# One tile's first layer in three products instead of one: a split chunk whose low part comes from an accumulating DMA

## The chip, the cores and the metric

The kernel runs on one core of a Trainium2 chip (trn2). The metric is the device time in microseconds of one execution; less is better. The core has five engines with queues of their own: PE (TensorE, matrix products), DVE (VectorE) and ACT (ScalarE) for elementwise work, POOL (GpSimd), and SP (SyncE), which here only issues DMAs. They are ordered by semaphores alone. Each engine works through its queue in order, so an instruction that waits holds up all behind it.

## What is computed

Three layers of a compressed interaction network over 512 samples, 32 fields and 64 embedding dimensions. Each layer multiplies its hidden rows with all rows of the input and mixes the products with a weight matrix:

```python
h, outs = x0, []
for i in range(3):
    Wk = Ws[i].reshape(128, h.shape[1], 32)
    xk = relu(einsum('bhd,bmd,ohm->bod', h, x0, Wk) + bs[i][None, :, None])
    if i != 2:
        outs.append(xk[:, :64])
        h = xk[:, 64:]
    else:
        outs.append(xk)
return concatenate([o.sum(axis=-1) for o in outs], axis=1)
```

All is float32. Layer 1 multiplies x0 with itself, so each pair of rows need be formed only once, with the two weights summed; layers 2 and 3 have 64 x 32 pairs.

## The kernel before

**Tiles.** The pairs (sample, dimension) are 32768 columns, cut into 64 tiles of T = 512. A chunk is 128 pairs of rows: 128 partitions by 512 columns, one contraction of PE. Layer 1 has five chunks (C1), layers 2 and 3 have sixteen each, handled in four groups of G = 4; one DVE instruction forms a group's products (128x2048).

**Stages.** The outer loop of every engine runs over i from 0 to 65. Step i does layer 1 of tile i, layer 2 of tile i - 1 and layer 3 of tile i - 2, in this order on PE. I call layer 1's group of four chunks A and its fifth chunk narrow, layer 2's groups B0 to B3 and layer 3's C0 to C3.

**Plain and split groups.** A plain group (A, B2, C2; L375 and L384) is multiplied as float32, for which the trace shows two matmul instructions per chunk. A split group (B0, B1, B3, C0, C1, C3) is multiplied in three float32r products, one matmul per chunk each. DVE writes the product into ZS (L221), ACT copies it rounded into ZH, the high part (L313), and the low part ZL = ZS - ZH is formed by POOL (L291), for B3 by DVE (L228). PE then adds low weight x high (L394), high weight x high (L397) and high weight x low (L400) into the same accumulator, waiting for the low part only ahead of L400.

**Slots.** ZS, ZH and ZL have three slots each (SSLOTS), given out in the order of the split groups. Group n may write ZS when the low part of group n - 3 is formed (L219), and ZH or ZL when PE has used group n - 3 (L311, L289). Plain groups share the two slots of ZW, X has four slots, XD (the row block that layer 1 multiplies X by) two.

**Between the layers.** ACT applies relu to the accumulator (layers 1 and 2: the hidden half to H at L329, the other half to R12 at L332; layer 3: L324). SP spreads H over the partitions with five DMAs (L145, L148), ACT copies it to PSUM (HP, L306), and DVE multiplies it with X. XD is likewise copied into XDP (L300). DVE sums R12 and R3 over the dimension (L237, L242).

**Order.** Each queue is written out by hand. ACT, step i: high B0, high B1, relu of layer 3 (tile i - 3), hidden copy for layer 3, high B3, copy of XD for tile i + 1, high C0, relu of layer 1, high C1, high C3, hidden copy for layer 2, relu of layer 2. DVE, step i: A's product, the narrow product, B0, B1, B2, B3, sum of R12, C0, low part of B3, C1, C2, C3, sum of R3. SP, step i: load XD and X for tile i + 1, spread layer 1's hidden rows of tile i, spread layer 2's of tile i - 1.

## Time and profile before

| | us |
|---|---|
| median of 3 runs (lowest, highest) | 1852.87 (1852.87, 1853.91) |
| the profiled execution | 1851.87 |
| its span, first to last instruction | 1850.1 |
| busy: PE, DVE, POOL, ACT | 1799.3, 1552.2, 1468.3, 1095.6 |
| mean granted clock of PE | 0.996 of full speed |

The span is what the rows below are read from; the profiled execution is 1.8 us longer than its span, and 1.0 below the median of the runs. A time of busy is the union of an engine's instructions, whatever they wait for inside. Matmuls are pipelined and overlap in the rows, so their distance in the chain of work, not their listed length, is what each costs.

### The profile page before, as it was taken

The page shows a single profiled execution, that of the slowest core. Times are in us where ns is not written, and L with a number is a line of the kernel's source. Part 1 is how long each engine was busy: PE and PEld are TensorE (multiplying, and loading weights), DVE is VectorE, ACT ScalarE, POOL GpSimd, SP SyncE. Part 2 cuts the span into 40 slices and gives each one's busy share as a digit, 9 for nine tenths or more (in the row PEclk, how much of TensorE's full clock was granted, in tenths as well). Part 3 has the DMA queues.
Part 4 walks back from the last instruction along what each step waited for, and adds up shares of the span by engine and source line. Part 5 has one row for each costly group of instructions (what it writes and reads, how often), then busy time and mean ns, then how long its engine had stood idle before and what let it go on. Part 6 is the DMA issues. An engine that isn't in the chain of part 4 may idle for free.

```text
span 1850.1 us, 18063 instructions
## 1 busy us (share of the span) xinstructions
PE 1799.3 (97%) x6284; PEld 1184.3 (64%) x6284; DVE 1552.2 (84%) x853; ACT 1095.6 (59%) x899; POOL 1468.3 (79%) x324
## 2 busy tenths in 40 slices
PE   3899999999999999999999999999999999999997
PEld 1566666666666666666666666666666666666665
DVE  3998898898898888888888888888888888988974
ACT  2566656656656666566565665665666666566562
POOL 0788878878878778778778778778778788788786
PEclk9999999999999999999999999999999999999998
DMA  8565455465465564564564564564564554654610
GB/s 201 111 123 121 98 122 116 101 125 114 100 128 107 105 128 105 106 129 103 107 129 102 109 128 99 114 128 93 121 128 92 122 125 92 125 122 95 126 26 20
DMA packets 119513, 205.83 MB, mean 111 GB/s; under 512 B 18816, under 2 KB 19968, under 8 KB 119424
## 3 DMA queue, kind: packets, MB, share of 16 engines
q1 hardware_dynamic: 119424, 204.68, 52.5%
q8 instruction: 51, 0.84, 0.2%
q14 instruction: 38, 0.31, 0.1%
HBM read 153.75 MB, written 0.52 MB: 83 GB/s over the span
## 4 chain that ended last, share of the span: by engine, by line
PE 96%; POOL 1%; DMA 1%; SPq 1%; ACT 1%; DVE 0%; issue 0%; DVEq 0%; POOLq 0%; ACTq 0%
PE ACC L384 24%; PE ACC L400 19%; PE ACC L394 19%; PE ACC L397 19%; PE ACC L375 12%; PE ACC L378 3%; POOL ZL L291 1%; DMA ZS<-in_w 1%; ACT ZH L313 0%; DVE ZS L221 0%; SPq L158 0%; DVE ZW L204 0%; ACT HP L306 0%; DMA H<-H 0%; SPq L139 0%
## 5 line engine op out<-in xcount | busy, mean ns | idle before, releaser
L291 POOL TENSOR_TENSOR ZL<-ZS,ZH 128x2048 fp32r<-128x2048 f32 x320 | 1468.1, 4617 | 372.8 <-ACT ZH L313 372.8
L313 ACT ACTIVATE ZH<-ZS 128x2048 fp32r<-128x2048 f32 x384 | 734.2, 1912 | 536.7 <-PE ACC L400 415.0
L221 DVE TENSOR_TENSOR ZS<-HP,X 128x2048 f32<-128x2048 f32 x384 | 870.5, 2281 | 150.9 <-ACT HP L306 149.6
L394 PE MATMUL ACC<-ZH,WL 128*128 128x512 f32 x1536 | 497.5, 446 | 7.3 <-ACT ZH L313 7.3
L384 PE MATMUL ACC<-ZW,WF 128*128 128x512 f32 x1024 | 460.2, 592 | 0.0
L400 PE MATMUL ACC<-ZL,WH 128*128 128x512 f32 x1536 | 421.7, 396 | 8.4 <-POOL ZL L291 8.3
L397 PE MATMUL ACC<-ZH,WH 128*128 128x512 f32 x1536 | 421.0, 396 | 0.0
L394 PEld LDWEIGHTS ACC<-ZH,WL 128*128 128x128 f32 x1536 | 289.9, 189 | 151.7 <-issue 98.9
L216 DVE TENSOR_TENSOR ZW<-HP,X 128x2048 f32<-128x2048 f32 x128 | 292.2, 2283 | 101.3 <-PE ACC L384 101.3
L400 PEld LDWEIGHTS ACC<-ZL,WH 128*128 128x128 f32 x1536 | 287.9, 188 | 81.6 <-POOL ZL L291 11.7
L397 PEld LDWEIGHTS ACC<-ZH,WH 128*128 128x128 f32 x1536 | 288.8, 188 | 70.2
L384 PEld LDWEIGHTS ACC<-ZW,WF 128*128 128x128 f32 x1024 | 194.0, 189 | 195.1 <-issue 183.7
L375 PE MATMUL ACC<-ZW,W 128*128 128x512 f32 x512 | 233.6, 599 | 30.8 <-DVE ZW L204 30.8
L375 PEld LDWEIGHTS ACC<-ZW,W 128*128 128x128 f32 x512 | 98.2, 192 | 131.1 <-issue 125.5
L204 DVE TENSOR_TENSOR ZW<-XDP,X 128x2048 f32<-128x2048 f32 x64 | 145.6, 2275 | 22.0 <-ACT XDP L300 18.0
L228 DVE TENSOR_TENSOR ZL<-ZS,ZH 128x2048 fp32r<-128x2048 f32 x64 | 157.7, 2464 | 1.4 <-ACT ZH L313 1.4
L324 ACT ACTIVATE R<-ACC,bias_sb 128x512 f32<-128x512 f32 x64 | 44.0, 688 | 170.4 <-PE ACC L400 170.4
L306 ACT ACTIVATE HP<-H 128x1024 f32<-128x1024 f32 x128 | 129.9, 1015 | 9.8 <-DMA H<-H 9.8
L329 ACT ACTIVATE H<-ACC,bias_sb 64x512 f32<-64x512 f32 x128 | 86.6, 676 | 9.4 <-PE ACC L378 5.1
L332 ACT ACTIVATE R<-ACC,bias_sb 64x512 f32<-64x512 f32 x128 | 87.5, 684 | 1.6
L378 PE MATMUL ACC<-ZN,W 128*128 128x512 f32 x128 | 65.4, 592 | 0.0
L237 DVE TENSOR_REDUCE S<-R 128x8 f32<-128x512 f32 (+1 forms) x65 | 43.9, 675 | 2.7 <-ACT R L332 2.7
(32 smaller groups left out, 165.0 us busy)
## 6 DMA issues: line engine op xcount, KB each, us to landing
X<-in_xpad SPq DMA_DIRECT2D x256, 512.0 KB, 9.0
H<-H SPq DMA_DIRECT2D x512, 64.0 KB, 2.0
XD<-in_xpad SPq DMA_DIRECT2D x256, 64.0 KB, 2.0
H<-H SPq DMA_DIRECT2D x128, 128.0 KB, 2.2
ZS<-in_w SPq DMA_DIRECT2D x6, 256.0 KB, 11.4
WF<-in_w SPq DMA_DIRECT2D x2, 256.0 KB, 11.9
out<-XD SPq DMA_DIRECT2D x4, 128.0 KB, 1.8
W<-in_w SPq DMA_DIRECT2D x1, 320.0 KB, 3.0
```

What stands on the lines that cost most here:

```text
L204: nc.vector.tensor_tensor(to, over(XDP[:, :], G), x[:, 0:G, :], ALU.mult).then_inc(wide_ready, 1)
L216: nc.vector.tensor_tensor(wide_slot(i, layer), h, x, ALU.mult).then_inc(wide_ready, 1)
L221: nc.vector.tensor_tensor(ZS[:, n % SSLOTS, :, :], h, x, ALU.mult).then_inc(prod_ready, 1)
L228: nc.vector.tensor_tensor(ZL[:, n % SSLOTS, :, :], ZS[:, n % SSLOTS, :, :], ZH[:, n % SSLOTS, :, :], ALU.subtract).then_inc(low_by_dve, 1)
L291: nc.gpsimd.tensor_tensor(ZL[:, n % SSLOTS, :, :], ZS[:, n % SSLOTS, :, :], ZH[:, n % SSLOTS, :, :], ALU.subtract).then_inc(low_by_pool, 1)
L306: nc.scalar.activation(HP[layer][:, :, :], H[layer][:, :, :], ACT.Copy).then_inc(h_copied[layer], 1)
L313: nc.scalar.activation(ZH[:, n % SSLOTS, :, :], ZS[:, n % SSLOTS, :, :], ACT.Copy).then_inc(high_ready, 1)
L375: last = nc.tensor.matmul(ACC[0][:, :], W1[:, g, :], ZW[:, n % WSLOTS, g, :], start=(g == 0), stop=False)
L384: last = nc.tensor.matmul(ACC[layer][:, :], WF[:, layer - 1, g, :], ZW[:, n % WSLOTS, g, :], start=False, stop=False)
L394: nc.tensor.matmul(ACC[layer][:, :], wl[:, g, :], ZH[:, n % SSLOTS, g, :], start=(k == 0 and g == 0), stop=False)
L397: nc.tensor.matmul(ACC[layer][:, :], wh[:, g, :], ZH[:, n % SSLOTS, g, :], start=False, stop=False)
L400: last = nc.tensor.matmul(ACC[layer][:, :], wh[:, g, :], ZL[:, n % SSLOTS, g, :], start=False, stop=(k == NS - 1 and g == G - 1))
```

## The change

Layer 1's group A becomes a split group. The weights W1 get a high part W1H (ACT) and a low part W1L (DVE) at the start. In each step PE multiplies W1L x ZH and W1H x ZH, then the narrow chunk as before, then waits for A's low part and multiplies W1H x ZL; relu of layer 1 now waits for that.

A's low part is formed in another way than the others. ACT writes ZH and then, from the same ZS, the negated high part into ZL (float32r, scale -1). POOL, ahead of its subtractions of the step, issues a DMA that adds ZS onto ZL in place (1 MB, 128 rows of 2048 elements). Its landing is counted in a semaphore of its slot, and PE, and the DVE product three groups later, wait for that.

There are now seven split groups in a step, A, B0, B1, B3, C0, C1, C3, over the same three slots. A wait on a low part is for that group's own former (POOL, DVE or DMA) rather than for all earlier ones. On ACT A's two copies stand at the head of the step. XD has one buffer in place of two, and SP loads X before XD and waits for XD's copy in between. The weights of layers 2 and 3 are staged in X's slots 2 and 3 in place of ZS, and the outputs in ZW in place of XD. The diff, cut to its core:

```diff
-PLAIN = 2
-SPLIT = (0, 1, 3)
-BY_DVE = ((1, 2),)
-NS = len(SPLIT)
+SPLIT = {0: (0,), 1: (0, 1, 3), 2: (0, 1, 3)}
+PLAIN = {0: (), 1: (2,), 2: (2,)}
+LOW_BY = {
+    (0, 0): "dma",
+    (1, 0): "pool", (1, 1): "pool", (1, 3): "dve",
+    (2, 0): "pool", (2, 1): "pool", (2, 3): "pool",
+}
+NS = 3
...
+        W1H, W1L = sb("W1H", [128, G, OUT], f32r), sb("W1L", [128, G, OUT], f32r)
...
-        XD = sb("XD", [128, 2, T])
+        XD = sb("XD", [128, T])
...
-        WS = ZS[:, 0:2, 0:NS, :].rearrange("p w n (g o) -> p w n g o", g=G)
-        OUTS = XD[:, :, :].rearrange("p a (b c) -> p (a b) c", b=2)
+        WS = X[:, 2:4, 0:NS, :].rearrange("p w n (g o) -> p w n g o", g=G)
+        OUTS = ZW[:, 0, 0:2, :].rearrange("p a (b c) -> p (a b) c", b=2)
...
+        def wait_low(engine, n):
+
+            if LOW_OF[n] == "pool":
+                engine.wait_ge(low_by_pool, LOW_COUNT[n])
+            elif LOW_OF[n] == "dma":
+                engine.wait_ge(low_by_dma[n % SSLOTS], 16 * LOW_IN_SLOT[n])
+            else:
+                engine.wait_ge(low_by_dve, LOW_COUNT[n])
...
                 t = i + 1
                 if live(t):
-                    if t >= 2:
-                        sp.wait_ge(xd_copied, t - 1)
+                    if t == 2:
+                        sp.wait_ge(w_low, 2)
+                    if t >= XSLOTS:
+                        sp.wait_ge(prod_ready, SPLIT_NO[t - XSLOTS + 2, 2, Q - 1] + 1)
+                    load_x(t)
+                    sp.wait_ge(xd_copied, t)
                     load_xd(t)
-                    if t >= XSLOTS:
-                        sp.wait_ge(prod_ready, split_before(t - XSLOTS + 2, 2, NS - 1) + 1)
-                    load_x(t)
...
-            dve.wait_ge(w1_summed, 4)
-
-            def wide_slot(i, layer):
-                n = wide_before(i, layer)
+            dve.wait_ge(w1_high, 1)
+            nc.vector.tensor_tensor(W1L[:, :, :], W1[:, 0:G, :], W1H[:, :, :], ALU.subtract).then_inc(w1_low, 1)
...
             def layer1(i):
                 x = X[:, i % XSLOTS, :, :]
-                to = wide_slot(i, 0)
+                n = SPLIT_NO[i, 0, 0]
+                if n >= SSLOTS:
+                    wait_low(dve, n - SSLOTS)
                 dve.wait_ge(xd_copied, i + 1)
                 dve.wait_ge(x_loaded[i % XSLOTS], 16 * NB * (i // XSLOTS + 1))
-                nc.vector.tensor_tensor(to, over(XDP[:, :], G), x[:, 0:G, :], ALU.mult).then_inc(wide_ready, 1)
+                nc.vector.tensor_tensor(ZS[:, n % SSLOTS, :, :], over(XDP[:, :], G), x[:, 0:G, :],
+                                        ALU.mult).then_inc(prod_ready, 1)
...
-                n = split_before(i, layer, SPLIT.index(q))
+                n = SPLIT_NO[i, layer, q]
                 if n >= SSLOTS:
-                    wait_lows(dve, n - SSLOTS + 1)
+                    wait_low(dve, n - SSLOTS)
                 nc.vector.tensor_tensor(ZS[:, n % SSLOTS, :, :], h, x, ALU.mult).then_inc(prod_ready, 1)
...
+                for layer in range(3):
+                    for q in SPLIT[layer] if live(i - layer) else ():
+                        n = SPLIT_NO[i, layer, q]
+                        if LOW_BY[layer, q] == "dma":
+                            pool.wait_ge(minus_ready, LOW_COUNT[n])
+                            pool.dma_start(ZL[:, n % SSLOTS, :, :], ZS[:, n % SSLOTS, :, :],
+                                           accum_op=ALU.add).then_inc(low_by_dma[n % SSLOTS], 16)
+                        if LOW_BY[layer, q] == "pool":
+                            if n >= SSLOTS:
+                                pool.wait_ge(split_used, n - SSLOTS + 1)
+                            pool.wait_ge(high_ready, n + 1)
+                            nc.gpsimd.tensor_tensor(ZL[:, n % SSLOTS, :, :], ZS[:, n % SSLOTS, :, :],
+                                                    ZH[:, n % SSLOTS, :, :], ALU.subtract).then_inc(low_by_pool, 1)
...
             def high(i, layer, q):
-                n = split_before(i, layer, SPLIT.index(q))
+                n = SPLIT_NO[i, layer, q]
                 if n >= SSLOTS:
                     act.wait_ge(split_used, n - SSLOTS + 1)
                 act.wait_ge(prod_ready, n + 1)
                 nc.scalar.activation(ZH[:, n % SSLOTS, :, :], ZS[:, n % SSLOTS, :, :], ACT.Copy).then_inc(high_ready, 1)
+                if LOW_OF[n] == "dma":
+                    nc.scalar.activation(ZL[:, n % SSLOTS, :, :], ZS[:, n % SSLOTS, :, :], ACT.Copy,
+                                         scale=-1.0).then_inc(minus_ready, 1)
 
             def relu(t, layer):
                 if layer == 0:
-                    act.wait_ge(narrow_used, t + 1)
+                    act.wait_ge(split_used, SPLIT_NO[t, 0, 0] + 1)
...
+            act.wait_ge(w1_summed, 4)
+            nc.scalar.activation(W1H[:, :, :], W1[:, 0:G, :], ACT.Copy).then_inc(w1_high, 1)
+            copy_xd(0)
             for w in range(2):
                 act.wait_ge(ws_loaded[w], 16 * NS)
                 nc.scalar.activation(WH[:, w, :, :, :], WS[:, w, :, :, :], ACT.Copy).then_inc(w_high, 1)
             act.wait_ge(small_loaded, 32)
-            copy_xd(0)
             for i in range(TILES + 2):
+                if live(i):
+                    high(i, 0, 0)
...
-                    pe.wait_ge(w1_summed, 4)
+                    pe.wait_ge(w1_low, 1)
                 else:
                     pe.wait_ge(relu_done[0], i)
-                n = wide_before(i, 0)
-                pe.wait_ge(wide_ready, n + 1)
-                for g in range(G):
-                    last = nc.tensor.matmul(ACC[0][:, :], W1[:, g, :], ZW[:, n % WSLOTS, g, :], start=(g == 0), stop=False)
-                last.then_inc(wide_used, 1)
+                n = SPLIT_NO[i, 0, 0]
+                pe.wait_ge(high_ready, n + 1)
+                for g in range(G):
+                    nc.tensor.matmul(ACC[0][:, :], W1L[:, g, :], ZH[:, n % SSLOTS, g, :], start=(g == 0), stop=False)
+                for g in range(G):
+                    nc.tensor.matmul(ACC[0][:, :], W1H[:, g, :], ZH[:, n % SSLOTS, g, :], start=False, stop=False)
                 pe.wait_ge(narrow_ready, i + 1)
-                nc.tensor.matmul(ACC[0][:, :], W1[:, G, :], ZN[:, :], start=False, stop=True).then_inc(narrow_used, 1)
-
-            def plain(i, layer):
-                n = wide_before(i, layer)
+                nc.tensor.matmul(ACC[0][:, :], W1[:, G, :], ZN[:, :], start=False, stop=False).then_inc(narrow_used, 1)
+                wait_low(pe, n)
+                for g in range(G):
+                    last = nc.tensor.matmul(ACC[0][:, :], W1H[:, g, :], ZL[:, n % SSLOTS, g, :],
+                                            start=False, stop=(g == G - 1))
+                last.then_inc(split_used, 1)
...
-                wait_lows(pe, n + 1)
+                wait_low(pe, n)
```

## Rows read from the trace of the kernel before

**Rows 1.** The page, part 1: busy us, share of the span, instructions of each engine.
```profile
PE 1799.3 (97%) x6284; PEld 1184.3 (64%) x6284; DVE 1552.2 (84%) x853; ACT 1095.6 (59%) x899; POOL 1468.3 (79%) x324
```

**Rows 2.** The chain that ended last, one period (start us, us, what).
```profile
903.32 3.43 PE ACC L375 x8
906.75 0.86 PE ACC L378 x2
907.61 0.92 PE ACC L394 x4
908.53 0.93 PE ACC L397 x4
...
913.20 3.43 PE ACC L384 x8
...
931.27 3.43 PE ACC L375 x8
```

**Rows 3.** The timeline of DVE (start us, us, engine line op, out<-in).
```profile
930.71 2.28 DVE L221 TENSOR_TENSOR ZS<-HP,X 128x2048 f32<-128x2048 f32 x1
932.91 0.68 DVE L237 TENSOR_REDUCE S<-R 128x8 f32<-128x512 f32 x1
...
942.38 2.27 DVE L221 TENSOR_TENSOR ZS<-HP,X 128x2048 f32<-128x2048 f32 x1
```

**Rows 4.** The timeline of ACT, the same columns, idle time before in brackets.
```profile
924.72 1.91 ACT L313 ACTIVATE ZH<-ZS 128x2048 fp32r<-128x2048 f32 x1 [1.11 <-DVE ZS L221]
...
933.09 1.91 ACT L313 ACTIVATE ZH<-ZS 128x2048 fp32r<-128x2048 f32 x1 [0.17 <-DVE ZS L221]
934.90 0.58 ACT L300 ACTIVATE XDP<-XD 128x512 f32<-128x512 f32 x1
...
947.42 1.92 ACT L313 ACTIVATE ZH<-ZS 128x2048 fp32r<-128x2048 f32 x1 [3.91 <-PE ACC L400]
949.24 1.01 ACT L306 ACTIVATE HP<-H 128x1024 f32<-128x1024 f32 x1
950.18 0.67 ACT L329 ACTIVATE H<-ACC,bias_sb 64x512 f32<-64x512 f32 x1
950.86 0.69 ACT L332 ACTIVATE R<-ACC,bias_sb 64x512 f32<-64x512 f32 x1
```

**Rows 5.** The timeline of POOL: the five subtractions of a period.
```profile
926.77 9.13 POOL L291 TENSOR_TENSOR ZL<-ZS,ZH 128x2048 fp32r<-128x2048 f32 x2 [0.52 <-ACT ZH L313]
940.45 13.73 POOL L291 TENSOR_TENSOR ZL<-ZS,ZH 128x2048 fp32r<-128x2048 f32 x3 [4.54 <-ACT ZH L313]
```

**Rows 6.** The timeline of SP's DMA queue, issues of a period.
```profile
923.63 0.50 SPq L145 DMA_DIRECT2D H<-H  x1
924.17 2.50 SPq L148 DMA_DIRECT2D H<-H  x4
926.71 2.40 SPq L139 DMA_DIRECT2D XD<-in_xpad  x4
929.15 1.90 SPq L134 DMA_DIRECT2D X<-in_xpad  x4
```

**Rows 7.** The page, part 6: DMA issues, KB each, median us to landing.
```profile
X<-in_xpad SPq DMA_DIRECT2D x256, 512.0 KB, 9.0
H<-H SPq DMA_DIRECT2D x512, 64.0 KB, 2.0
```

**Rows 8.** Windows: busy by engine, PE's clock, DMA share, GB/s.
```profile
930.00:940.00 10.00, 10.00 (x36) 6.52 (x35) 10.00 (x6) 5.62 (x5) 5.90 (x2) 1.00 1.01 202
933.00:937.00 4.00, 4.00 (x13) 2.28 (x13) 4.00 (x3) 2.40 (x2) 2.90 (x1) 1.00 1.07 209
```

**Rows 9.** The start on PE: timeline, then a window with the granted clock.
```profile
26.78 5.33 PE L375 MATMUL ACC<-ZW,W 128*128 128x512 f32 x8 [26.78 <-DVE ZW L204]
...
37.03 5.32 PE L375 MATMUL ACC<-ZW,W 128*128 128x512 f32 x8 [4.07 <-DVE ZW L204]
...
45.40 1.10 PE L397 MATMUL ACC<-ZH,WH 128*128 128x512 f32 x4
48.96 1.20 PE L400 MATMUL ACC<-ZL,WH 128*128 128x512 f32 x4 [2.46 <-POOL ZL L291]
...
37.00:40.40 3.40, 3.37 (x4) 1.52 (x5) 0.87 (x2) 1.03 (x1) 0.00 (x0) 0.51 0.48 121
```

More of the change, by code:

```diff
@@ L34, in live, with in_order @@
     return 0 <= t < TILES
-def wide_before(i, layer):
-    n = sum(live(k - l) for k in range(i) for l in range(3))
-    return n + sum(live(i - l) for l in range(layer))
-def split_before(i, layer, k):
-    n = NS * sum(live(s - l) for s in range(i) for l in (1, 2))
-    return n + NS * sum(live(i - l) for l in range(1, layer)) + k
-def lows_before(n, by_dve):
-    order = [(layer, k) for i in range(TILES + 2) for layer in (1, 2) if live(i - layer) for k in range(NS)]
-    return sum((u in BY_DVE) == by_dve for u in order[:n])
+def in_order(which):
+    return {g: n for n, g in enumerate(
+        (i, layer, q) for i in range(TILES + 2) for layer in range(3) if live(i - layer) for q in which[layer])}
+SPLIT_NO, PLAIN_NO = in_order(SPLIT), in_order(PLAIN)
+LOW_OF = [LOW_BY[layer, q] for _, layer, q in SPLIT_NO]
+LOW_COUNT = [LOW_OF[:n + 1].count(LOW_OF[n]) for n in range(len(LOW_OF))]
+LOW_IN_SLOT = [LOW_OF[n % SSLOTS:n + 1:SSLOTS].count(LOW_OF[n]) for n in range(len(LOW_OF))]
 def cin_kernel(nc, xpad, w1, w1t, w2, w3, bias, ident_in, out):
@@ L102, in cin_kernel @@
         small_loaded = sem("small_loaded")
-        w1_summed, w_high, w_low = sem("w1_summed"), sem("w_high"), sem("w_low")
+        w1_summed, w1_high, w1_low = sem("w1_summed"), sem("w1_high"), sem("w1_low")
+        w_high, w_low = sem("w_high"), sem("w_low")
         cleared = sem("cleared")
         x_loaded = [sem(f"x_loaded{n}") for n in range(XSLOTS)]
-        xd_loaded = [sem(f"xd_loaded{n}") for n in range(2)]
+        xd_loaded = sem("xd_loaded")
         xd_copied = sem("xd_copied")
@@ L114, in cin_kernel @@
         low_by_pool, low_by_dve = sem("low_by_pool"), sem("low_by_dve")
+        minus_ready, low_by_dma = sem("minus_ready"), [sem(f"low_by_dma{n}") for n in range(SSLOTS)]
         relu_done = [sem(f"relu_done{n}") for n in range(3)]
@@ L261, in _ @@
                 if live(i - 1):
-                    for q in range(Q):
+                    product(i, 1, 0)
+                if live(i - 1):
+                    for q in range(1, Q):
                         product(i, 1, q)
@@ L268, in _ @@
                 if live(i - 1):
-                    low(i, 1, 2)
+                    low(i, 1, 3)
                 if live(i - 2):
@@ L428, in _ @@
                                 turn(n)
-                        if q == PLAIN:
-                            plain(i, layer)
+                        if q in PLAIN[layer]:
+                            plain(i, layer, q)
                         else:
```

45 lines of the change are left out of this document (17 added, 28 removed).

## The prediction

> **What bounds the kernel now.** I read the page's busy shares first: PE is busy for 97% of the span, DVE for 84%, POOL for 79%, ACT for 59% [rows 1]. A share alone proves nothing, so next the chain that ended last, in order of time [rows 2]: one period, from the start of one layer 1 group to the next, is 931.27 - 903.32 = 27.95 us, and every piece in it is PE. Layer 1 takes 3.43 for A and 0.86 for the narrow chunk; each split chunk takes 3 x 0.93 = 2.80; each plain chunk takes 3.43. Check: 4.29 + 6 x 2.80 + 2 x 3.43 = 27.95, to the rounding of the pieces. Nothing waits for ACT, DVE, POOL or a DMA in the steady state. So two questions decide the change: what it takes from PE, and whether the other engines can still stay ahead of PE.
>
> **What it takes from PE.** A turns from a plain chunk (3.43) into a split one (2.80): 0.63 less, a period of 27.32. Over 64 tiles that is 40 us, and a profiled execution of 1851.9 - 40 = 1812 if PE stays the bound.
>
> **What it adds elsewhere, per tile.** ACT: one high copy and one negated copy of 128x2048, 1.9 each [rows 4], 3.8 in all on an engine busy for 59%. POOL: one DMA issue, queued ahead of B0's subtraction; its five subtractions take 5 x 4.6 = 23 [rows 5]. DVE: nothing in sum. The DMA engines: 1 MB more, summed onto what is there. By throughput all of it fits into 27.32. By latency it does not, and that is where I put the result.
>
> **The new loop.** PE waits for A's low part in the middle of layer 1. That wait alone would be harmless if the DMA began early. But DVE waits for the same landing: there are three split slots, B3 is three groups behind A, so B3's product may overwrite ZS only when the DMA has read A's. Queued behind B3's product on DVE are sum12, C0's product, B3's subtraction, C1, the plain chunk of layer 3 and C3. I follow it from one landing to the next:
> - landing to the start of B3's product: 0.10, the lag with which ACT followed a product of DVE (930.71 + 2.28 = 932.99, ACT at 933.09) [rows 3, 4].
> - B3's product to the end of C3's product, gapless on DVE: 942.38 + 2.27 - 930.71 = 13.94 [rows 3].
> - 0.10 again, then ACT in its written order: C3's high copy, layer 2's hidden copy, two relus: from 947.42 to 951.55, less 0.09 by which starts overlap ends, 4.04 [rows 4].
> - A's high copy 1.81 (933.09 to 934.90, a start to a start), then the negated copy 1.91 [rows 4].
> - ACT to POOL: 926.77 behind 924.72 + 1.91 = 926.63, 0.14 [rows 4, 5].
> The sum is 22.04 us. With L for the time from POOL's release to the landing, the period is the larger of 27.32 and 22.04 + L. PE remains the bound only if L is at most 5.3; the kernel of before is met at L = 5.9. On this path the next A's product is no obstacle: it is ready 0.6 + 2.3 behind C3's product, A's high copy begins 4.1 behind it. POOL is not either, but by little: C3's high copy ends 2.0 behind C3's product, POOL's subtraction 4.6 + 0.1 later, 6.7 against 7.9 for the negated copy.
>
> **L, which no row shows.** No DMA of the trace adds, and POOL issues none. From below: a small SBUF to SBUF DMA (H, 64 KB) lands 2.0 after its issue [rows 7], and 1.05 MB at the highest rate that a long window shows, 209 GB/s [rows 8], takes 5.0: 7.0. From above: a sum reads two operands, so twice 5.0, and the X load of 2.1 MB ahead of it takes another 10.0: 22.0. That load is there every time. SP begins to spread layer 2's hidden rows right behind the relus (923.63) and needs 3.1 for it (to 926.71) [rows 6]; then, by the new order, X. The relus end 18.2 behind the landing, so X is issued from 21.3 on, the accumulating DMA at 22.0. Of X the trace says that it fills the DMA engines for some ten microseconds (share 1.01 in 930 to 940) [rows 8], and that each of its four 512 KB DMAs lands 9.0 after its issue [rows 7]. I take L = 10.0: nearest to that row, since the new DMA joins the same crowd, with 1.0 more because it is twice as long, reads twice and has its descriptors written by POOL, less what its fewer, longer rows save. Period: 32.0.
>
> A page speaks against the change here. The Trainium skill, "Collectives: The Full Stack", section "The bandwidth ceiling: the fold count and why AG ≠ RS ≠ AR", says that a reducing transfer runs at half the rate of a copy since it reads two sources; "DMA: Bandwidth & Descriptors", section "Issuing engines are not separate DMA queues", says that transfers of POOL and SP interleave on the same 16 engines. Together they would put L near 20, no run so far shows either, and the estimate goes by the rows.
>
> **Two further terms.** XD is now loaded behind X and not ahead of it: issued at 21.3 + 1.9 = 23.2 to 25.6 [rows 6], it lands when the engines have moved X, the new DMA (1.05 to 2.1 MB) and itself (0.26 MB): 3.4 to 4.5 MB at 209 GB/s, 16 to 21 behind 21.3, so at 38 to 43, or 6 to 11 behind the next landing. ACT wants to copy it at 4.3. C0's high copy is queued behind that, then three subtractions of POOL. At 6 they end at 6 + 0.6 + 1.9 + 0.1 + 13.8 = 22.4, in line with the 22.04; at 11, 5 later, spread over the two periods that this loop spans. Second, PE idles 32 - 27.3 = 4.7 per tile. At 33 to 37, before the second tile, it idled 4.1, and then the granted clock was 0.51, which is the 1.2 GHz level, for 3.4 us; the eight matmuls took 5.32 instead of 3.60. After 2.5 us of idle time at 46.5 to 49.0 it stayed at full speed [rows 9]. That costs PE 1.7 per tile, and PE is 12.8 from the landing to the end of B3 (0.93 + 2 x 2.80 + 3.43 + 2.80) where C3's high copy has 14.0 to 14.1: 0.4 shows. The two overlap; I add 0.8 for both. Period 32.8.
>
> **Sum.** 64 x (32.8 - 27.95) = 310. The start differs too (high and low part of W1, XD copied before the other weights, X slots 2 and 3 lent to weights): in the trace of before PE began at 26.8 behind XD's copy [rows 9], so it can begin sooner, but A's low part lands some ten later; 0, within 10. Profiled: 1851.9 + 310 = 2162; the median of the runs of before lies 1.0 above its profiled one: **2163 us**, 17% slower.
>
> **The rivals**, with time = 1852.9 + 64 x (period - 27.95).
> - Forecast: L from 8.5 to 13, periods 30.5 to 35.8, 2016 to 2355: 0.50.
> - PE stays the bound, the other side: the accumulating DMA lands within 5.3, period 27.32, 1812. For it: rows of 8 KB against X's 2 KB may move faster than any row shows, and nothing was measured on POOL's queue. Against it: 3.3 us for 1.05 MB is 318 GB/s, 1.5 times the best window, beside the X load. 0.06. The Trainium skill, "DMA: Bandwidth & Descriptors", section "Anatomy of one DMA — SWDGE (gpsimd) path", fits 2.0 us plus bytes over 436 GB/s, an estimate of 4.4 us for this DMA if it were alone and a plain copy: by that rule this rival would hold. The rows speak against it.
> - A quick DMA that is hardly disturbed, L from 5.3 to 8.5 (7.0 is the lower bound): periods 27.4 to 30.5, 1853 to 2016; at 7.0, 1923. For it: few long rows, round robin with X. 0.24, of which 0.04 within 0.2%, and that little only near L = 5.9.
> - The DMA bears both loads, L from 13 to 22: 2355 to 2900. For it: the engines' share is already 1.01 beside X. 0.20.
> The 80% range leaves out what lies under L = 7 and over 15 or so with the XD term: **1900 to 2480**. A measurement of this kernel can tell 0.2% (4 us) from no change: faster 0.06, same 0.04, slower 0.90.
>
> **What would show it.** In the profile after: the chain of waits turns from pure PE to DMA ZL, DVE ZS, ACT ZH and the negated copy in turn; PE's busy share falls to 27.3 / 32.8 = 83% or, at the lower clock in places, a little above; PE's line for layer 1's low part waits for the DMA in each tile for some 4 to 5 us; DVE's B3 product begins 0.1 behind the landing and 13.9 lies between it and the end of C3's; the issues list the new DMA with 8.5 to 13 us to landing; the granted clock falls after the wait; ACT waits for XD. I would be wrong if that DMA lands in under 6 us, or if B3's product doesn't wait for it.

## The result, and the profile after

The changed kernel takes 2443.61 us (median of four runs, 2435.77 to 2446.73) against 1852.87: a ratio of 1.318, with an interval of 1.3166 to 1.3198. The profiled execution took 2445.9, with a span of 2444.1 and a mean granted clock of 0.873, where before showed 0.996. The direction and the range held; the middle was 280 us too low, and the time lies above the forecast's own case (2016 to 2355), in the rival to which the prediction gave 0.20.

The page of after, part 1 (to be read against [rows 1]), the clock line of part 2, the shares of the chain that ended last in part 4, and one group of part 5:
```profile
PE 1913.8 (78%) x6540; PEld 1330.4 (54%) x6540; DVE 1549.0 (63%) x854; ACT 1330.7 (54%) x1028; POOL 1518.5 (62%) x388
...
PEclk8789889888888898898898888888998988889999
...
DMA 36%; DVE 24%; issue 15%; ACT 13%; PE 8%; SPq 2%; POOL 2%; DVEq 0%; ACTq 0%; POOLq 0%
...
L402 PE MATMUL ACC<-ZL,W1H 128*128 128x512 f32 x256 | 131.3, 664 | 477.9 <-DMA ZL<-ZS 477.9
```
DVE has as much work as before, POOL 50 us and ACT 235 us more, and all of them have much idle time: no engine's throughput is the bound. PE waited 477.9 us for the DMA, 7.5 in each of the 64 tiles, ahead of layer 1's low part; and its matmuls run longer at a granted clock of eight and nine tenths along the whole kernel. The chain that ended last, all PE in [rows 2], now lies with the DMA for 36% of the span and with PE for 8%. In the waits of the whole run, the longest on the DMA is DVE's (us in total, times, longest), ahead of B3's product:
```profile
DVE ZS L229 <- DMA ZL<-ZS: 665.3, 63, 17.1
```

Part 6, DMA issues (count, KB each, median us to landing), which answers [rows 7]:
```profile
X<-in_xpad SPq DMA_DIRECT2D x256, 512.0 KB, 11.4
ZL<-ZS POOLq DMA_DIRECT2D x64, 1024.0 KB, 13.7
...
XD<-in_xpad SPq DMA_DIRECT2D x256, 64.0 KB, 14.3
```

One period in the timelines of after, DVE, ACT, POOL, SP and PE, which answer [rows 3 to 6]:
```profile
1220.44 2.29 DVE L229 TENSOR_TENSOR ZS<-HP,X 128x2048 f32<-128x2048 f32 x1 [9.35 <-DMA ZL<-ZS]
1232.04 2.28 DVE L229 TENSOR_TENSOR ZS<-HP,X 128x2048 f32<-128x2048 f32 x1
```
```profile
1234.82 1.92 ACT L326 ACTIVATE ZH<-ZS 128x2048 fp32r<-128x2048 f32 x1 [2.88 <-PE ACC L426]
...
1238.98 1.92 ACT L326 ACTIVATE ZH<-ZS 128x2048 fp32r<-128x2048 f32 x1
1240.80 1.89 ACT L328 ACTIVATE ZL<-ZS 128x2048 fp32r<-128x2048 f32 x1
```
```profile
1207.93 0.88 POOL L298 DMA_DIRECT2D ZL<-ZS  x1 [1.36 <-ACT ZL L328]
1227.93 13.76 POOL L304 TENSOR_TENSOR ZL<-ZS,ZH 128x2048 fp32r<-128x2048 f32 x3 [9.27 <-ACT ZH L326]
1242.99 0.87 POOL L298 DMA_DIRECT2D ZL<-ZS  x1 [1.30 <-ACT ZL L328]
```
```profile
1207.22 2.10 SPq L137 DMA_DIRECT2D X<-in_xpad  x4
...
1242.06 2.09 SPq L137 DMA_DIRECT2D X<-in_xpad  x4
```
```profile
1220.46 2.08 PE L402 MATMUL ACC<-ZL,W1H 128*128 128x512 f32 x4 [6.18 <-DMA ZL<-ZS]
```
This is the loop of the prediction. POOL issues the DMA at 1207.93; it lands some 12.5 us later and releases two engines at once, DVE for B3's product (1220.44) and PE for A's low part (1220.46). DVE reaches C3's product at 1232.04, ACT makes C3's high copy at 1234.82, the hidden copy, two relus, A's high copy and the negated copy, and POOL issues the next DMA at 1242.99. X's load goes out 0.7 and 0.9 ahead of POOL's DMA in these two.

All experiments are compared by three numbers, each a mean over the 300 to 1700 us of the span: P, the distance of two DMAs of POOL; L, from such a DMA's issue to the start of the product B3 that waits for it; and gap, P less L, from that start to the next issue. After has P = 37.26, L = 13.66 (10.36 to 15.09) and gap = 23.60. Before has P = 27.95. Where the first packet of POOL's DMA is named, it is the first one that the trace has of POOL's queue behind the issue, again a mean over these tiles.

### The profile page after: what moved, and what is told of

Same layout as the page of the kernel before. It is cut to its first block, busy times and chain, and to the rows that moved or that the text cites. A ratio compares the mean times of both kernels' runs of the same rounds, so it can differ in the third digit from the quotient of the medians.

```text
span 2444.1 us, 18200 instructions
## 1 busy us (share of the span) xinstructions
PE 1913.8 (78%) x6540; PEld 1330.4 (54%) x6540; DVE 1549.0 (63%) x854; ACT 1330.7 (54%) x1028; POOL 1518.5 (62%) x388
## 4 chain that ended last, share of the span: by engine, by line
DMA 36%; DVE 24%; issue 15%; ACT 13%; PE 8%; SPq 2%; POOL 2%; DVEq 0%; ACTq 0%; POOLq 0%
DMA ZL<-ZS 34%; DVE ZS L229 8%; DVE ZL L236 5%; DVE ZW L224 5%; ACT ZL L328 5%; DVE ZS L211 4%; ACT ZH L326 3%; ACT HP L319 2%; PE ACC L420 2%; POOL ZL L304 2%; PE ACC L410 2%; PE ACC L426 2%; PE ACC L423 2%; ACT R L348 2%; ACT H L345 1%
## 5 line engine op out<-in xcount | busy, mean ns | idle before, releaser
L326 ACT ACTIVATE ZH<-ZS 128x2048 fp32r<-128x2048 f32 x448 | 856.5, 1912 | 1029.5 <-DVE ZS L229 591.8
L402 PE MATMUL ACC<-ZL,W1H 128*128 128x512 f32 x256 | 131.3, 664 | 477.9 <-DMA ZL<-ZS 477.9
L423 PE MATMUL ACC<-ZH,WH 128*128 128x512 f32 x1536 | 455.8, 422 | 0.0
L420 PEld LDWEIGHTS ACC<-ZH,WL 128*128 128x128 f32 x1536 | 324.3, 211 | 138.6 <-issue 64.4
L402 PEld LDWEIGHTS ACC<-ZL,W1H 128*128 128x128 f32 x256 | 73.4, 317 | 544.4 <-DMA ZL<-ZS 532.4
L423 PEld LDWEIGHTS ACC<-ZH,WH 128*128 128x128 f32 x1536 | 318.2, 207 | 81.2
L211 DVE TENSOR_TENSOR ZS<-XDP,X 128x2048 f32<-128x2048 f32 x64 | 146.0, 2281 | 19.2 <-ACT XDP L313 9.9
L298 POOL DMA_DIRECT2D ZL<-ZS x64 | 56.2, 879 | 154.2 <-ACT ZL L328 151.9
L328 ACT ACTIVATE ZL<-ZS 128x2048 fp32r<-128x2048 f32 x64 | 121.2, 1894 | 0.0
L395 PE MATMUL ACC<-ZH,W1L 128*128 128x512 f32 x256 | 72.8, 407 | 38.3 <-ACT ZH L326 38.3
## 6 DMA issues: line engine op xcount, KB each, us to landing
ZL<-ZS POOLq DMA_DIRECT2D x64, 1024.0 KB, 13.7
XD<-in_xpad SPq DMA_DIRECT2D x256, 64.0 KB, 14.3
```

The source lines that it names most:

```text
L211: nc.vector.tensor_tensor(ZS[:, n % SSLOTS, :, :], over(XDP[:, :], G), x[:, 0:G, :], ALU.mult).then_inc(prod_ready, 1)
L326: nc.scalar.activation(ZH[:, n % SSLOTS, :, :], ZS[:, n % SSLOTS, :, :], ACT.Copy).then_inc(high_ready, 1)
L328: nc.scalar.activation(ZL[:, n % SSLOTS, :, :], ZS[:, n % SSLOTS, :, :], ACT.Copy, scale=-1.0).then_inc(minus_ready, 1)
L402: last = nc.tensor.matmul(ACC[0][:, :], W1H[:, g, :], ZL[:, n % SSLOTS, g, :], start=False, stop=(g == G - 1))
L420: nc.tensor.matmul(ACC[layer][:, :], wl[:, g, :], ZH[:, n % SSLOTS, g, :], start=(k == 0 and g == 0), stop=False)
L423: nc.tensor.matmul(ACC[layer][:, :], wh[:, g, :], ZH[:, n % SSLOTS, g, :], start=False, stop=False)
```

## The experiments

The kernel before took 1852.4 to 1853.1 (medians) beside all of them. Under each expectation stand the time in us, its ratio to the kernel before with the interval, and the mean granted clock where it bears on the case. SP's order decides what is on the DMA engines with POOL's DMA, so the first three change what SP issues when, and nothing else.

### XD ahead of X

```
+                    sp.wait_ge(xd_copied, t)
+                    load_xd(t)
                     if t == 2:
                         sp.wait_ge(w_low, 2)
...
                     load_x(t)
-                    sp.wait_ge(xd_copied, t)
-                    load_xd(t)
```

> Undoes one part: SP loads XD ahead of X again (one buffer as in the changed kernel). Theory (the loop from one landing of A's DMA to the next is some 22.6 us of DVE and ACT work plus 13 to 14 us of DMA, and the late XD adds about 1 us per tile on average by holding up ACT): XD lands in about 2 us, ACT never waits for it, the DMA still takes 13 to 14 us beside X; period 36.3 us, total 2380 to 2410. Rival (XD behind X is most of what exceeds the forecast of 32.8): total near 2200. Rival (XD is irrelevant): 2440.

2114.86 us, 1.141 (1.138 to 1.1446), clock 0.942. Neither theory came near. P 31.78, L 8.96, gap 22.83: what moved is L. Part 6 of its page, then a DMA of POOL and the X load beside it:
```profile
X<-in_xpad SPq DMA_DIRECT2D x256, 512.0 KB, 12.2
ZL<-ZS POOLq DMA_DIRECT2D x64, 1024.0 KB, 8.9
XD<-in_xpad SPq DMA_DIRECT2D x256, 64.0 KB, 2.0
```
```profile
1228.42 0.88 POOL L298 DMA_DIRECT2D ZL<-ZS  x1 [1.38 <-ACT ZL L328]
```
```profile
1231.28 4.28 SPq L137 DMA_DIRECT2D X<-in_xpad  x4
```
XD's issues take SP's time, so X goes out 2.9 us behind POOL's DMA and not 0.7 to 0.9 ahead of it. The bytes are the same; the DMA lands 4.7 sooner and X only 0.8 later.

What the order does stands in the packets. These are the queues in a window (packets, MB, share of the 16 engines; q0 is POOL's queue, q1 SP's): after from POOL's issue at 1207.93 to 1213, then from 1213 to 1220; then this run from 1229.5 to 1236.5, behind the issue at 1228.42:
```profile
q1 hardware_dynamic: 506, 0.97, 92.3%
...
q0 software_dynamic: 144, 1.05, 72.4%
q1 hardware_dynamic: 300, 0.58, 31.9%
```
```profile
q0 software_dynamic: 140, 1.05, 87.1%
q1 hardware_dynamic: 158, 0.24, 10.8%
```
In this period of after not one packet of POOL's DMA runs in the first 5 us: X's packets have the engines. Once POOL's run, they have most of them. Here POOL's packets run first and X's come behind. The first packet of POOL's DMA runs 5.98 us behind its issue in after and 1.48 behind it here; from there to the landing it takes 7.7 and 7.45. So 4.5 of the 4.7 is time ahead of the first packet.

XD now lands in 2.0 rather than 14.3. Two things changed at once, XD's place and X's; the next run takes them apart.

### XD early, X in its old place

```
                     load_x(t)
-                    sp.wait_ge(xd_copied, t)
-                    load_xd(t)
+                    if t == 1:
+                        sp.wait_ge(xd_copied, t)
+                        load_xd(t)
                 if live(i):
                     spread_hidden(i, 0)
+                if live(i + 2):
+                    sp.wait_ge(xd_copied, i + 2)
+                    load_xd(i + 2)
                 if live(i - 1):
```

> XD of the tile after next is loaded between the two spreads, well ahead; X keeps exactly its place of the changed kernel, behind the last spread, some 0.7 us before POOL's DMA. Tells apart the two things that loading XD first changed (XD early, X 4 us later than POOL's DMA). Theory (the time to landing is set by how much of X is queued on the DMA engines ahead of the accumulating DMA): still 13 to 14 us to landing, ACT waits for XD no more, period about 36.3, total 2370 to 2410. Rival (the late XD is what cost, through ACT): near the 2115 of the kernel that loads XD first.

2443.62, 1.319 (1.3165 to 1.3218), no different from after. P 37.19, L 13.74, gap 23.45. Part 6, and an issue of POOL with the X load that it meets:
```profile
ZL<-ZS POOLq DMA_DIRECT2D x64, 1024.0 KB, 13.8
XD<-in_xpad SPq DMA_DIRECT2D x256, 64.0 KB, 1.9
```
```profile
1244.81 0.87 POOL L302 DMA_DIRECT2D ZL<-ZS  x1 [1.38 <-ACT ZL L332]
```
```profile
1243.88 2.09 SPq L137 DMA_DIRECT2D X<-in_xpad  x4
```
XD lands 12 us sooner and it is worth nothing; X is 0.9 ahead as in after, and L is as in after. So in the changed kernel the late XD has no price, and the place of X has all of it. Of the theory the landing came, 13 to 14 us; the gain that it still expected from an early XD didn't.

### X behind the landing

The kernel "XD ahead of X" and ahead of X's load a wait for the landing of A's low part:

```
                     load_xd(t)
...
+                    n = SPLIT_NO[i, 0, 0]
+                    sp.wait_ge(low_by_dma[n % SSLOTS], 16 * LOW_IN_SLOT[n])
                     load_x(t)
```

> XD ahead of X, and SP loads X only when A's low part has landed, so that the accumulating DMA has the engines to itself. Theory (about 6 us of the 13.7 are the X load beside it; its own share of the engines, 13.3% of 2444 us over 64, is 5.1 us, with 0.9 on POOL and some 2 to land): 8 us to landing, period 22.6 + 8 = 30.6, total 2025 within 40. Rival (the accumulating DMA is slow by itself, whatever runs beside it): 12 to 14 us to landing, total 2290 to 2420.

1979.07, 1.068 (1.0649 to 1.0711), clock 0.974. P 29.63, L 7.35 (7.16 to 8.51), gap 22.29. The DMA has the engines nearly to itself; L has shrunk to near the prediction's lower bound, 7.0, and hardly scatters. The first packet runs 1.49 behind the issue, as in the run before, so the 1.6 that L loses lie behind it. The time is a little under what the theory allowed, 2025 within 40, for it had 8 for L. DVE waits for the later X ahead of A's product, 37.6 us in all, but that is off the loop: the steps from the landing to the next issue take as long as before.

### The sum left out of the DMA

After's kernel with a plain copy in the place of the accumulating one; A's low part is then the product itself and not the difference.

```
-                            pool.dma_start(ZL[:, n % SSLOTS, :, :], ZS[:, n % SSLOTS, :, :],
-                                           accum_op=ALU.add).then_inc(low_by_dma[n % SSLOTS], 16)
+                            pool.dma_start(ZL[:, n % SSLOTS, :, :], ZS[:, n % SSLOTS, :, :]).then_inc(low_by_dma[n % SSLOTS], 16)
```

> The same DMA from POOL's queue without the sum: a converting copy of ZS onto ZL, so that A's low part is wrong (ZS itself in place of ZS minus its high part); all else as in the changed kernel, X beside it included. Theory A (an accumulating DMA costs twice a copy on the engines, since it reads two operands): 2.5 us less of the engines' time, with X beside it 3 to 5 less to landing, total 2150 to 2260. Theory B (the time is set by sharing the engines with X, the sum itself costs little): within 1 us of 13.7, total 2380 to 2450.

2266.65 (one run). P 34.46, L 11.22: nearer to Theory A, though the landing gained 2.4 and not 3 to 5. Then the same edit on the kernel "X behind the landing":

> The kernel with X behind the landing, and the DMA a converting copy without the sum (A's low part is wrong). Tells the price of the sum with nothing beside it. With the sum the DMA lands 7.35 us after POOL's release. Theory (the engines' time per DMA was 5.1 with the sum and 3.5 without, in the shares of their queue): 5.8 to landing, period 28.1, total 1865 within 15. Rival (the sum costs only beside X, or the latency hides it): 7 and 1960 to 1980. Rival (reading two operands doubles the time on the engines): 4.9, PE becomes the bound, 1815 to 1830.

1863.72, 1.006 (1.0037 to 1.0081). P 27.90, L 5.02 (4.69 to 5.68), gap 22.87. Its page, and that of "X behind the landing" with the sum, POOL's issues in part 6 and its queue in part 3, first the copy, then the sum:
```profile
ZL<-ZS POOLq DMA_DIRECT2D x64, 1024.0 KB, 4.9
...
q0 software_dynamic: 9216, 67.11, 9.6%
```
```profile
ZL<-ZS POOLq DMA_DIRECT2D x64, 1024.0 KB, 7.2
...
q0 software_dynamic: 9216, 67.11, 16.7%
```
The copy lands 2.35 us sooner. Per DMA the queue holds the 16 engines for 16.7% of 1978.3 / 64 = 5.16 us with the sum, for 9.6% of 1861.8 / 64 = 2.79 without: 1.85 times. Beside X the sum costs about as much, 13.66 - 11.22 = 2.44. With L = 5.02, under the 5.3 that the prediction asked for, the period is back at that of before, 27.90.

It is not the 27.32 of a pure PE period, so the expectation's rival, 4.9 and PE as the bound, had the landing right and the bound wrong. The loop still sets the period: DVE waits for the landing ahead of B3's product in every tile, 1.7 us on average. It has become longer, from 22.29 to 22.87. The row that grew is DVE's subtraction for B3, which stands on the loop (300 to 1700 us, first "X behind the landing", then the copy; busy, mean ns of one):
```profile
L238 DVE TENSOR_TENSOR ZL<-ZS,ZH 128x2048 fp32r<-128x2048 f32 x48 | 109.5, 2281 | 0.0
```
```profile
L238 DVE TENSOR_TENSOR ZL<-ZS,ZH 128x2048 fp32r<-128x2048 f32 x50 | 150.1, 3003 | 0.0
```
In the shorter period it meets a subtraction of POOL in each tile, and takes 0.72 longer; the runs without a DMA, below, show the same at full size. And although the period is that of before, the time is 11 us longer. In the PE timeline, the second tile's layer 1 begins at 49.22 where that of before began at 37.03 [rows 9]:
```profile
49.22 2.04 PE L396 MATMUL ACC<-ZH,W1L 128*128 128x512 f32 x4 [15.80 <-ACT ZH L327]
```

### PE kept busy with zeros

After's kernel; PE multiplies by a weight of zeros 24 times ahead of its wait for A's low part, into the same accumulator.

```
+                for g in range(24):
+                    nc.tensor.matmul(ACC[0][:, :], W0[:, :], ZH[:, n % SSLOTS, g % G, :], start=False, stop=False)
                 wait_low(pe, n)
```

> The changed kernel with 24 matmuls of zero weights (5.6 us of PE at full clock) ahead of PE's wait for A's low part; they add nothing to the sum. In the changed kernel the loop less the DMA is 23.6 us on average where 22.04 were counted; the smallest stretches are 22.6. Theory (the difference is PE at its lower clock level after 6 to 7 us without work: B3 is used late, and C3's high copy waits for that): the granted clock stays up, the stretch falls to 22.3 to 22.8, total 2360 to 2395. Rival (the clock is off the path, something else stretches the loop): 2440 as before.

2384.34 (2370.75 and 2397.93), 1.287 (1.2769 to 1.2969), clock 0.969. P 36.18, L 13.62, gap 22.54. Windows across the end of the wait, of after and then with the zeros (window; busy PE, PEld, DVE, ACT, POOL; granted clock; DMA share; GB/s):
```profile
1216.00:1218.00 2.00, 0.00 (x0) 0.00 (x0) 0.00 (x0) 0.00 (x0) 2.00 (x1) 0.63 0.94 213
1218.00:1220.00 2.00, 0.00 (x0) 0.00 (x0) 0.00 (x0) 0.00 (x0) 0.65 (x1) 0.50 0.97 241
1220.00:1222.00 2.00, 1.54 (x4) 1.25 (x5) 1.56 (x1) 0.00 (x0) 0.00 (x0) 0.50 1.08 203
```
```profile
1216.00:1218.00 2.00, 2.00 (x10) 1.59 (x10) 0.00 (x0) 0.00 (x0) 2.00 (x1) 1.00 1.07 242
1220.00:1222.00 2.00, 1.89 (x8) 1.57 (x9) 1.91 (x1) 0.00 (x0) 0.00 (x0) 1.00 1.08 198
```
In after the granted clock is down to 0.50, the 1.2 GHz level, by the end of PE's wait, and the four matmuls of the low part take 2.08; with the zeros it stays at 1.00 and four take 1.20. L stays as it was, the gap loses 1.06, and all of it at one place: from the end of C3's product to C3's high copy, which waits for PE to be done with B3, it is 1.54 in after and 0.48 with the zeros. So the clock has a price of 1.06 us per tile, although PE's throughput is not what bounds the kernel. The two runs lie 27 us apart and the profile is of the faster; by the medians the price is 0.93 per tile, by the two profiled runs 1.17.

### No DMA at all

After's kernel; POOL issues nothing and everybody who waited for the landing waits for the negated copy, so A's low part is the negated product and nothing is added to it.

```
-                engine.wait_ge(low_by_dma[n % SSLOTS], 16 * LOW_IN_SLOT[n])
+                engine.wait_ge(minus_ready, LOW_COUNT[n])
...
-                            pool.wait_ge(minus_ready, LOW_COUNT[n])
-                            pool.dma_start(ZL[:, n % SSLOTS, :, :], ZS[:, n % SSLOTS, :, :],
-                                           accum_op=ALU.add).then_inc(low_by_dma[n % SSLOTS], 16)
+                            continue
```

> The DMA is left out: PE and DVE wait for the negated copy alone, so A's low part is minus its high part. All else stays, the order of XD and X included. Theory (without the DMA the loop is 22.0 to 22.6 us, below PE's 27.32): PE is the bound again, 1812 within 10. Rival (ACT's extra copies, the late XD or the order of waits hold PE up as well): 1830 to 1950.

1873.22, 1.011 (1.008 to 1.0138). The theory, a PE bound of 1812, fell. The waits over 300 to 1700 (us in total, times, longest):
```profile
ACT XDP L311 <- DMA XD<-in_xpad: 154.5, 50, 4.1
DVE ZS L229 <- POOL ZL L302: 188.3, 99, 2.2
```
With the loop gone the next two things show: ACT waits 154.5 / 50 = 3.1 us for XD, which is behind X, in nearly each tile, and DVE waits for POOL's low parts. That XD is the cause is read from these rows and the chain; I didn't undo it in this kernel.

### Three ways to shorten the loop

**A fourth ZS slot.** X behind the landing, XD first; a fourth slot for ZS alone, so that B3's product no longer waits for A's DMA; ZW is down to one slot to make room; A's low matmuls come behind B1's on PE, and ACT makes A's copies and B0's high copy ahead of layer 2's relus.

```
-XSLOTS, WSLOTS, SSLOTS = 4, 2, 3
+XSLOTS, WSLOTS, SSLOTS = 4, 1, 3
+ZSLOTS = 4
...
-                if n >= SSLOTS:
-                    wait_low(dve, n - SSLOTS)
+                if n >= ZSLOTS:
+                    wait_low(dve, n - ZSLOTS)
```

> Cuts the loop from landing to landing, keeping the accumulating DMA: four ZS slots (and one ZW slot to make room), so that no product of DVE waits for the landing; PE multiplies A's low part behind B1 in place of at once; ACT forms A's high and negated copies ahead of layer 2's relu; XD first, X behind the landing. Theory (nothing but this loop made the changed kernel slow; then PE is the bound with a period of 27.3): 1812 to 1840. Rival (the fifteen engine microseconds of DMA, the extra copies and POOL's five subtractions behind the DMA collide somewhere anyway): 1860 to 1950.

2053.91, 1.109 (1.107 to 1.1107), outside both expectations and worse than three slots. Its waits over 300 to 1700:
```profile
ACT HP L328 <- DMA H<-H: 168.8, 46, 4.7
DVE ZS L238 <- ACT HP L328: 219.5, 46, 5.8
```
The landing isn't waited for, but a new loop is: PE uses B1's low part, then A's, only then is B3's high copy free to overwrite A's slot, and DVE's subtraction and four products stand behind that copy. The hidden copy waits 3.7 for H in each tile. Several edits are mixed in this run, and it says only that this order is worse, not which edit made it so.

**Copies earlier.** X behind the landing, and on ACT the negated copy first, then A's high copy, both ahead of layer 2's relus:

```
-                nc.scalar.activation(ZH[:, n % SSLOTS, :, :], ZS[:, n % SSLOTS, :, :], ACT.Copy).then_inc(high_ready, 1)
                 if LOW_OF[n] == "dma":
                     nc.scalar.activation(ZL[:, n % SSLOTS, :, :], ZS[:, n % SSLOTS, :, :], ACT.Copy,
                                          scale=-1.0).then_inc(minus_ready, 1)
+                nc.scalar.activation(ZH[:, n % SSLOTS, :, :], ZS[:, n % SSLOTS, :, :], ACT.Copy).then_inc(high_ready, 1)
...
                     copy_hidden(i, 0)
+                if live(i + 1):
+                    high(i + 1, 0, 0)
                 if live(i - 1):
                     relu(i - 1, 1)
```

> The kernel with XD first and X behind the landing, and on ACT the negated copy ahead of A's high copy, both ahead of layer 2's relus: the DMA is released 1.8 + 1.4 us earlier in the loop. Theory: ACT's part of the loop falls from 22.3 to 19.1, but POOL's queue takes over, whose subtraction for C3 stands ahead of the DMA: landing, 0.1, 13.9, 0.1, high copy 1.9, 0.1, 4.6, then 7.35: period 28.1, total 1862 within 15; the trace shows POOL's DMA released right behind a subtraction, without idle time. Rival (the loop is ACT's alone): PE becomes the bound, 1812 to 1825. Rival (the later relus hold up layer 3): 1880 to 1960.

1916.63, 1.034 (1.0325 to 1.0362), the quickest kernel with the DMA that computes everything. P 28.75, L 7.56, gap 21.19: 1.10 less than the 22.29 of "X behind the landing", where the changed order promised 1.81 (A's high copy out of the way) + 0.67 + 0.68 (two relus). Its rows of POOL:
```profile
1209.14 5.45 POOL L307 TENSOR_TENSOR ZL<-ZS,ZH 128x2048 fp32r<-128x2048 f32 x1 [1.17 <-ACT ZH L332]
1214.78 9.21 POOL L307 TENSOR_TENSOR ZL<-ZS,ZH 128x2048 fp32r<-128x2048 f32 x2 [0.19 <-issue]
1223.93 0.84 POOL L301 DMA_DIRECT2D ZL<-ZS  x1
```
POOL's DMA now follows its C3 subtraction without a pause, and POOL's three subtractions for C0, C1 and C3 follow each other without one in every tile: they begin 7.3 behind the start of B3's product, when C0's high copy is made, and take 13.9, together the gap of 21.19. The negated copy is ready 1.7 ahead of the issue. So the path through ACT has been cut below the path through POOL, which lay 1.2 beneath it in "X behind the landing", and the rest of what was promised is gone there. The expectation had looked for POOL's path through C3's high copy alone, 20.7. In the rows the first subtraction takes 5.45, beside one of DVE's, where 4.6 was usual. The later relus, the rival, aren't what binds: ACT does wait for H, 143.4 us over 300 to 1700, but POOL's first subtraction begins as soon behind the landing as before.

**The DMA ahead of C3's subtraction.** The same, with POOL issuing the DMA for the next tile ahead of the subtraction for C3:

```
+                        if (layer, q) == (2, 3) and live(i + 1):
+                            add(i + 1)
...
-                        if LOW_BY[layer, q] == "dma":
-                            pool.wait_ge(minus_ready, LOW_COUNT[n])
-                            pool.dma_start(ZL[:, n % SSLOTS, :, :], ZS[:, n % SSLOTS, :, :],
-                                           accum_op=ALU.add).then_inc(low_by_dma[n % SSLOTS], 16)
```

> The kernel with early copies, and POOL issues A's DMA ahead of C3's subtraction. Before this edit the DMA was issued right behind that subtraction, 21.2 us behind the landing. Theory (POOL's order is what bound that kernel): the release falls to 19 to 20 behind the landing, the period to 27.3 to 28.0, total 1812 to 1860, faster than or equal to the kernel before. Rival (C3's subtraction, now behind, holds up B1's product and POOL's next subtractions by as much as it gives): 1880 to 1920.

1926.96, 1.040 (1.038 to 1.0415). No engine waits for the DMA any more, and it is still slower. The waits over 300 to 1700, and a DMA of POOL:
```profile
DVE ZS L232 <- POOL ZL L314: 246.0, 49, 5.3
POOL ZL L298 <- ACT ZL L337: 123.4, 49, 2.8
```
```profile
1200.84 0.88 POOL L298 DMA_DIRECT2D ZL<-ZS  x1 [2.52 <-ACT ZL L337]
```
POOL waits 2.5 per tile for the negated copy with C3's subtraction queued behind that wait, and DVE's product for B1 waits 246.0 / 49 = 5.0 for this low part. The wait has moved to another engine, as the rival said; the period is 28.87.

### The low part without a DMA

A's low part as a sixth subtraction of POOL, XD first, no negated copy:

```
-    (0, 0): "dma",
+    (0, 0): "pool",
```

> No DMA and no negated copy: POOL forms A's low part by a sixth subtraction; XD first. Theory: POOL becomes the bound, 6 x 4.6 = 27.6 us per tile plus the gaps of waiting for high copies, period 27.7 to 28.2, total 1835 to 1870. Rival (PE still is): 1812.

1953.47, 1.054 (1.0528 to 1.056). Part 1 of its page, and the subtractions' groups by form (shortest / median / longest ns): those of DVE and of POOL here, then DVE's in before:
```profile
PE 1793.2 (92%) x6540; PEld 1223.9 (63%) x6540; DVE 1683.4 (86%) x854; ACT 1218.6 (62%) x964; POOL 1883.8 (97%) x388
```
```profile
L236 DVE TENSOR_TENSOR ZL<-ZS,ZH x64: 4020/4383/6728, 49.1 to 1900.2; 128x2048 fp32r<-128x2048 f32 x64
...
L304 POOL TENSOR_TENSOR ZL<-ZS,ZH x384: 4517/4635/6637, 25.3 to 1936.8; 128x2048 fp32r<-128x2048 f32 x192
```
```profile
L228 DVE TENSOR_TENSOR ZL<-ZS,ZH x64: 2343/2358/4718, 50.9 to 1801.5; 128x2048 fp32r<-128x2048 f32 x64
```
POOL is full. Six times its 4.6 of before are 27.6, but a subtraction that shares its time with DVE's takes up to 6.6, and DVE's takes 4.38 where it took 2.36. The period is 29.5, and neither the theory's 28.2 nor PE's bound came.

Sharing A's low part out, even steps to POOL and odd steps to DVE behind B1's product:

```
-LOW_OF = [LOW_BY[layer, q] for _, layer, q in SPLIT_NO]
+LOW_OF = [("pool", "dve")[i % 2] if layer == 0 else LOW_BY[layer, q] for i, layer, q in SPLIT_NO]
```

> As the kernel with six subtractions on POOL, but A's low part is formed by POOL in even steps and by DVE, behind B1's product, in odd ones: POOL 25.3 and DVE 26.1 us per tile on average. Theory (throughput then allows PE's 27.32): 1812 to 1845. Rival (three slots are too few to even out the steps): 1850 to 1900.

2002.0, 1.081 (1.0791 to 1.0823). Worse again, beyond the rival's 1900 too, though POOL has half a subtraction less. I didn't take this one apart further.

No version made is quicker than the kernel before.

## Why the prediction held and where its terms were off

**The loop was right.** PE's wait for A's low part, B3's product held by the same landing, and from there DVE, ACT, the negated copy: all of it stands in the rows of after in the order given. Shortening L alone shows it: take L from 13.66 to 8.96, 7.35 and 5.02 and P goes from 37.26 to 31.78, 29.63 and 27.90. P less L, the loop's own part, moves little beside that: 23.60, 22.83, 22.29 and 22.87. The first three shrink as PE's wait and its lower clock shrink; the last grows by DVE's slower subtraction.

**The range held, the middle didn't, and the step that missed is the size of L.** The prediction took 10.0, "nearest to that row, since the new DMA joins the same crowd", with 1.0 for its length, its two reads and its descriptors, and gave 0.20 to the case in which the DMA bears both loads, from 13 up. 13.66 came, and with it that case: the range was wide enough for it, the forecast's own case was not. The runs price the parts:

| | L | what it adds | issue to first packet |
|---|---|---|---|
| copy, X behind the landing | 5.02 | | 1.15 |
| with the sum | 7.35 | 2.35 | 1.49 |
| X 2.9 behind the issue | 8.96 | 1.6 | 1.48 |
| X 0.7 to 0.9 ahead of it | 13.66 | 4.7 | 5.98 |

Each X DMA landed 9.0 after its issue [rows 7] with nothing of weight beside it. The new DMA comes behind four of these with a megabyte of its own, and that was worth not 1.0 more but 4.7. "Joins the same crowd" was the wrong picture: it doesn't share the engines with X from the start, its first packet comes only when SP's queue has moved another 1.2 MB (the mean), somewhat more than half of X. The lower bound, 2.0 plus 1.05 MB at 209 GB/s, gave 7.0 and 7.35 is what the DMA takes undisturbed, but for a wrong reason: the copy takes 5.02, well under it. The bound's rate came from windows in which X filled the engines with rows of 2 KB; a bound taken from another transfer's rate isn't a bound. The Trainium skill, "Collectives: The Full Stack", section "The bandwidth ceiling: the fold count and why AG ≠ RS ≠ AR", has a reducing transfer at half the rate: by that rule, 2.00 times the engines' time where 1.85 was measured. What it left open is that the latency grows by less, 5.02 to 7.35. The prediction's estimate by the Trainium skill, "DMA: Bandwidth & Descriptors", section "Anatomy of one DMA — SWDGE (gpsimd) path", 4.4 us for a copy alone, lies 0.6 under the measured 5.02; the rival built on it, that PE stays the bound, needed a DMA without sum and without company, and even with that the loop held the period, at 27.90.

**The 22.04 us of the loop.** The loop's own part, taken apart in the timelines (means over the same tiles, us; the sums agree with the gaps to 0.02):

| from the start of B3's product | counted | after | with zeros | X behind the landing | the copy |
|---|---|---|---|---|---|
| to the end of C3's product | 13.94 | 13.88 | 13.88 | 13.88 | 14.61 |
| to C3's high copy | 0.10 | 1.54 | 0.48 | 0.26 | 0.10 |
| to the end of the negated copy | 7.76 | 7.88 | 7.87 | 7.87 | 7.87 |
| to POOL's issue | 0.14 | 0.30 | 0.30 | 0.30 | 0.30 |
| sum | 21.94 | 23.60 | 22.53 | 22.31 | 22.88 |

With the 0.10 from the landing to B3's product the prediction had 22.04; that step is 0.02 and is in L here. So the count is right to 0.2 where nothing else waits. It leaves out two things: C3's high copy waits for PE, which comes late and at the lower clock (1.4 of after's 1.54), and DVE's subtraction takes longer where it meets one of POOL's (the copy's run).

**The clock.** Predicted: PE's part of the loop 14.4 against 14.0 through DVE and ACT, 0.4 shows. In after PE takes 1234.78 - 1220.46 = 14.3 in the quoted period and 15.0 in the next, and both times C3's high copy waited for it: at 1234.82 its product had been there for 0.5 (1232.04 + 2.28), at 1271.54 for 1.1. In the mean of all periods C3's high copy comes 1.44 later than DVE alone would let it, and the zeros took away 1.06 of that. The prediction took one price at the 1.2 GHz level, 1.7 for eight matmuls of a plain group [rows 9], and had no row for how far behind the wait the lower clock would last.

**XD.** Predicted: up to 5 over two periods, and a part of 0.8 per tile. Measured: nothing in this kernel (the run "XD early"). It did arrive later than before, but no later than the loop could bear; where the loop was gone, in the run without a DMA, ACT waited 3.1 for it per tile.

**The start.** Predicted 0, within 10. In the copy's run, whose period is that of before, the span is 11.7 longer, and 64 x 0.05 more of it was saved by the period: 15 us for start and end. In after it is hidden: the first two periods are 24.6 and 32.7, shorter than the rest, and 1850.1 + 64 x 9.31 = 2446 stands against 2444.1.

**The sum.** 4.42 us per tile are missing: L 3.66, the clock and what else the gap held 0.76 (23.60 against 22.04 + 0.8). 64 x 4.42 = 283, and the miss is 281. One printed number of the rivals doesn't follow from its working: a period of 27.4 gives 1818, not the 1853 at which the quick DMA's case begins; 1853 belongs to 27.95. And the upper end of the forecast's case, 2355, holds the 0.8 of the two further terms, which its lower end, 2016, doesn't. Of the signs named beforehand, the chain, DVE's start right behind the landing (0.02, where 0.1 was named), PE's wait (4 to 5 were named, 7.5 came) and the lower clock came; PE's share of 83% did not (78%, for the longer period), nor ACT's wait for XD as a price.

**What stays open.** Why the packets of POOL's DMA wait for so much of a load that was issued 0.7 to 0.9 us ahead of them was measured and is not explained, and no run has X between 0.9 ahead and 2.9 behind. PE's own period of 27.32 was reached in no run. The versions with a fourth slot and with the shared low part were not taken apart.

## What to carry to other kernels

A transfer in the place of an instruction frees an engine and puts its latency on whatever waits for it; before counting bytes, count who waits for the landing, and whether one of those feeds the next issue. Then look at what another queue issues just ahead of it, since that can have the engines first: the order of SP's two loads was worth 330 us here, without a byte changed. And when a loop is cut, price what lies just beneath it: here POOL's path lay 1.2 beneath the one through ACT, and most of the gain ended there.
